# Fourteen expert steps of the second layer moved into the later groups of the second attention

## The reference, cut to what matters

```python
# attention, 16 heads of 8 rows a batch; q, k, v are (b, h, dh=8, t=256) views of the projections
attn = softmax(einsum('bhdt,bhds->bhts', k, v) * temperature)
out  = einsum('bhdt,bhts->bhds', q, attn)
x = x + ga * out
h = layernorm(x) * (1 + cb) + sb
# experts: 8 routed and one shared, 176 hidden rows each; two experts a token are weighted, the rest 0
g = einsum('th,ehi->eti', h, w_gate); u = einsum('th,ehi->eti', h, w_up)
eo = einsum('eti,eih->eth', silu(g) * u, w_down)
x = x + gb * (einsum('te,eth->th', combine, eo) + sigmoid(h @ shared_gate) * so)
```

## Time and profile before

| | |
|---|---|
| median of three runs | 473.43 us |
| profiled execution | 476.3 us |
| its span | 474.5 us, 7765 instructions |
| TensorE products, busy | 426.4 us, 90% |
| VectorE, busy | 360.9 us, 76% |
| ScalarE, busy | 336.2 us, 71% |
| GpSimd, busy | 252.9 us, 53% |
| mean granted TensorE clock | 0.845 |

### The profile page before, as it was taken

The page is one execution under the profiler, slowest core; times in us unless marked ns, Lnnn a source line. Parts: engine busy times, 40 slices in busy tenths (PEclk is TensorE's granted clock), DMA queues, the critical chain, the costliest instruction groups (busy, mean ns, idle before and its releaser), DMA issues.

```text
span 474.5 us, 7765 instructions
## 1 busy us (share of the span) xinstructions
PE 426.4 (90%) x2212; PEld 285.5 (60%) x2212; DVE 360.9 (76%) x891; ACT 336.2 (71%) x898; POOL 252.9 (53%) x276
## 2 busy tenths in 40 slices
PE   8979778899899899886999889969989999999995
PEld 6667666676567677652433335324447887787883
DVE  4766795867898879689858896995848777879763
ACT  3364558787688686778998889968946566585552
POOL 3302238786866776822443543443418964766663
PEclk9997998999999999995565555555569999999999
DMA  6730021121134643633058344203114342433640
GB/s 185 207 112 2 0 79 57 44 92 56 35 114 108 164 149 103 123 87 114 12 90 118 96 98 131 60 5 102 24 22 149 127 126 81 141 128 92 183 130 22
DMA packets 45675, 44.68 MB, mean 94 GB/s; under 512 B 5557, under 2 KB 33789, under 8 KB 45633
## 3 DMA queue, kind: packets, MB, share of 16 engines
q1 hardware_dynamic: 45632, 44.19, 34.5%
HBM read 37.73 MB, written 6.44 MB: 93 GB/s over the span
## 4 chain that ended last, share of the span: by engine, by line
PE 43%; DVE 13%; issue 5%; ACT 3%; POOL 1%; POOLq 0%; DVEq 0%; ACTq 0%
PE P L1244 8%; PE P L1245 8%; PE P L1246 8%; PE P L1523 8%; PE P L1513 5%; DVE nm L902 4%; PE P L1380 1%; ACT EX L1179 1%; POOL hidl L469 1%; PE P L1349 1%; PE P L1268 1%; DVE O L917 1%; PE P L1374 1%; DVE kvs L697 1%; DVE SC L606 1%
## 5 line engine op out<-in xcount | busy, mean ns | idle before, releaser
L469 POOL TENSOR_TENSOR hidl<-tmp,hidh 128x512 fp32r<-128x512 f32 x116 | 149.3, 1296 | 76.6 <-ACT hidh L1131 73.9
L1179 ACT ACTIVATE EX<-P,nm 128x256 f32<-128x256 f32 x256 | 116.9, 496 | 12.5 <-DVE nm L902 12.2
L1131 ACT ACTIVATE hidh<-tmp 128x512 fp32r<-128x512 f32 x116 | 73.1, 630 | 44.8 <-DVE tmp L865 20.4
L902 DVE TENSOR_REDUCE nm<-P 128x4 f32<-128x1024 f32 x64 | 77.8, 1218 | 24.4 <-PE P L1513 24.0
L1523 PE MATMUL P<-EX,qs 128*32 128x256 f32 x512 | 66.8, 619 | 12.1 <-DVE O L917 12.0
L1244 PE MATMUL P<-XH,WH 128*128 128x512 f32 x176 | 76.1, 433 | 1.5 <-DVE tmp L974 0.6
L1245 PE MATMUL P<-XH,WL 128*128 128x512 f32 x176 | 70.1, 399 | 0.0
L1246 PE MATMUL P<-XL,WH 128*128 128x512 f32 x176 | 70.1, 398 | 0.0
L513 POOL TENSOR_TENSOR qs<-qT,rz 128x128 f32<-128x128 f32 x64 | 24.6, 406 | 81.5 <-DVE rz L910 81.5
L865 DVE TENSOR_TENSOR tmp<-P,G 128x512 f32<-128x512 f32 x64 | 43.6, 687 | 25.2 <-ACT P L1152 20.1
L1244 PE MATMUL P<-hidh,WH 128*128 128x512 f32 x124 | 50.7, 409 | 11.3 <-POOL hidl L469 9.8
(11 more groups left out here) (138 smaller groups left out, 670.7 us busy)
## 6 DMA issues: line engine op xcount, KB each, us to landing
G<-gate_rows SPq DMA_DIRECT2D x56, 256.0 KB, 3.3
kv_parts<-kvs SPq DMA_DIRECT2D x16, 256.0 KB, 2.4
VS<-kv_parts SPq DMA_DIRECT2D x48, 64.0 KB
KS<-kv_parts SPq DMA_DIRECT2D x48, 64.0 KB
G<-gate_rows SPq DMA_DIRECT2D x8, 224.0 KB, 3.0
G<-gate_rows SPq DMA_DIRECT2D x8, 192.0 KB, 3.3
G<-gate_rows SPq DMA_DIRECT2D x8, 160.0 KB, 2.6
X<-in_x SPq DMA_DIRECT2D x4, 256.0 KB, 2.9
```

Of the source, the lines that this page charges most:

```text
L469: nc.gpsimd.tensor_tensor(hidl[:, u % 3, :], source, hidh[:, u % 3, :].bitcast(fp32), ALU.subtract).then_inc(s["low_ready"], 1)
L902: v.tensor_reduce(nm1[:, g % 4, 2 * h:2 * h + 2, :], P[:, bank:bank + 2, :].rearrange("p j (h s) -> p (j h) s", h=2), AX.X, ALU.max, negat ...
L1131: sc.activation(hidh[:, u % 3, :], source, ACT.Copy).then_inc(s["high_ready"], 1)
L1179: last = sc.activation(ex1(g, j)[:, h * S:(h + 1) * S], P[:, bank_s1(g, j), h * S:(h + 1) * S], ACT.Exp, bias=nm1[:, g % 4, j, h:h + 1], a ...
```

## The change

Groups 18 to 31 of the attention (from GF = 18) each take one expert step along; MERGED = 14 steps, all 13 of pair 0 and the first of pair 1. In these steps SiLU is written as (tanh(g/2) + 1) x g x 0.5 and then times up: a tanh on ScalarE (`tanh1`) and two three-operand instructions on VectorE (`silu1`, `up1`), the multiplication with the router's weight on GpSimd (`gated`), and the down product as one product in full fp32 (`down_whole`, with the staged weights and without split). From group 18 on the scores have four banks, one for each j, and the maxima are taken bank by bank (`maxima1`, four a group in place of two); banks 4 and 7 are for gate and up. Copies of the context go to ScalarE from group 16 on. To be ready, the weight loads and splits move forward (quarters at groups 2 to 5, 7 to 10, 12 to 15), and so do the layer norm and the router of pairs 0 and 1 (13 to 18 in place of 15 to 25). The other 38 steps stay as they were, behind the attention. `exps_ready`, `maxima_done`, `used1` and `split1` hold the new counts.

```diff
 LAG = 4
+GF = 18
...
+
+        hidf = EX[:, 0, 0:2, :]
...
+        spare = [kvs[:, r, :, :].rearrange("p o d -> p (o d)").bitcast(fp32) for r in range(KVR)]
+        th = spare[0:2]
+        t1 = spare[2]
+        hidm = [spare[3], kvf[:, :, :, :].rearrange("p k o d -> p (k o d)")]
...
             load_experts_1(0)
+            load_experts_1(1)
             attention_out(0)
             kv_load(2)
-            load_experts_1(1)
+            load_experts_1(2)
             attention_out(1)
             kv_store(3)
             attention_out(2)
             kv_load(3)
-            load_experts_1(2)
-            attention_out(3)
-            attention_out(B - 4)
-            attention_out(B - 3)
             gates_store(NP)
             for n in range(GR):
                 gate_load(NP * E + n)
-            attention_out(B - 2)
-            attention_out(B - 1)
+            attention_out(3)
             for n in range(GR, NP * C1):
                 p, i = divmod(n, C1)
-                if p == 0 and i == 9:
-                    gates_store(NP + 1)
-                if p >= 2 and i == 0:
+                if n in (6, 10, 14, 18):
+                    attention_out(B - 4 + n // 4 - 1)
+                if i == 0:
                     gates_store(NP + p)
                 gate_load(NP * E + n)
...
+            def gated(m):
+
...
+                pool.wait_ge(s["u_read"], m + 1)
+                pool.wait_ge(gate_in[q % GR], gates_loaded(q))
+                if m >= 2:
+                    pool.wait_ge(s["down_done"], NP * STEPS0 + m - 1)
+                nc.gpsimd.tensor_tensor(hidm[m % 2], t2[:, m % 2, :], G[:, q % GR, :], ALU.mult
+                                        ).then_inc(s["bc_read"], 1)
...
-                if g in (15, 15 + GPP):
-                    root(3, (g - 15) // GPP)
+                if g in (13, 13 + GPP):
+                    root(3, (g - 13) // GPP)
                 queries(g)
...
-                    clear(1)
...
+                for w, quarters in enumerate(((2, 3, 4, 5), (7, 8, 9, 10), (12, 13, 14, 15))):
...
+                    clear(g // 5)
+                for p in range(3):
                     i = g - GPP * p
-                    if i in (10, 12):
...
+                    if i in (9, 11):
+                        attention_residual(2 * p + (i - 9) // 2)
+                    if i == 15 and p < 2:
...
+                if g >= GF:
+                    gated(g - GF)
+            root(3, 2)
+            for n in range(MERGED, NP * C1):
                 p, i = divmod(n, C1)
-                low_part(NP * STEPS0 + n, hidf[:, n % 2, :])
...
+            def maxima1(g, j):
+
+                dve.wait_ge(s["s1_ps"], HPG * g + j + 1)
+                v.tensor_reduce(nm1[:, g % 4, j, :], P[:, bank_s1(g, j), :].rearrange("p (h s) -> p h s", h=2),
+                                AX.X, ALU.max, negate=True).then_inc(s["nm1_ready"], 1)
+
+            def silu1(m):
+
+                dve.wait_ge(s["gact_ready"], m + 1)
+                v.scalar_tensor_tensor(out=t1, in0=th[m % 2], scalar=1.0, in1=P[:, BANK_GM, :],
+                                       op0=ALU.add, op1=ALU.mult).then_inc(s["t1_done"], 1)
+
+            def up1(m):
+
+                dve.wait_ge(s["t1_done"], m + 1)
+                dve.wait_ge(s["u_ps"], m + 1)
+                if m >= 2:
+                    dve.wait_ge(s["bc_read"], used1(m - 1))
+                v.scalar_tensor_tensor(out=t2[:, m % 2, :], in0=t1, scalar=0.5, in1=P[:, BANK_UM, :],
+                                       op0=ALU.mult, op1=ALU.mult).then_inc(s["u_read"], 1)
+
             def denominators(g):
                 dve.wait_ge(s["e1_ready"], HPG * (g + 1))
...
+                if 3 <= g < GF:
                     outputs(g - 3)
-                if g + 1 < NG:
+                if g + 1 < GF:
                     maxima(g + 1, 0)
+                elif g + 1 < NG:
+                    maxima1(g + 1, 0)
                 if g == 0:
                     gate_experts(0, NP - 1)
                 if g >= 1:
                     denominators(g - 1)
+                if g > GF:
+                    silu1(g - 1 - GF)
+                if GF <= g + 1 < NG:
+                    maxima1(g + 1, 1)
+                if g > GF:
+                    up1(g - 1 - GF)
+                if GF <= g + 1 < NG:
+                    maxima1(g + 1, 2)
                 if g < 2:
                     kv(2 * TPP + 2 + g)
                 if g == 2:
...
-                    kv((NP - 1) * TPP + (10, 11, 13, 14).index(g))
+                if g in (9, 10, 12, 15):
...
+                    if i == 13:
                         ln_stats(3, p)
+                    if i == 14:
+                        ln_apply(3, p)
+                    if i == 18:
+                        router_weights(1, p, 2)
+                if g == NG - 1:
+                    ln_stats(3, 2)
+                if g + 1 < GF:
+                    maxima(g + 1, 1)
+                elif g + 1 < NG:
+                    maxima1(g + 1, 3)
+                for p in range(2):
+                    i = g - GPP * p
...
                         router_logits(1, p)
...
+                    if i == 17:
+                        router_weights(1, p, 0)
+                        router_weights(1, p, 1)
             denominators(NG - 1)
...
+            silu1(MERGED - 1)
+            up1(MERGED - 1)
...
+            dve.wait_ge(s["c1_ps"], NG - 3)
+            dve.wait_ge(s["bc_read"], used1(MERGED))
+            for n in range(MERGED, NP * C1):
...
+            def outputs(g):
+                b = g // GPB
+                act.wait_ge(s["c1_ps"], g + 1)
...
+                sc.activation(O[:, b % 2, g % GPB, :], P[:, BANK_C1, 0:S], ACT.Copy).then_inc(s["o1_ready"], 1)
+
+            def tanh1(m):
...
+                act.wait_ge(s["g_ps"], m + 1)
...
+                    act.wait_ge(s["t1_done"], m - 1)
+                sc.activation(th[m % 2], P[:, BANK_GM, :], ACT.Tanh, scale=0.5).then_inc(s["gact_ready"], 1)
...
+                    if j == 0 and g in (17, 17 + GPP):
+                        router_exp(1, (g - 17) // GPP)
+                    if j == 1 and g >= GF - 1:
+                        outputs(g - 2)
                     if j == HPG - 1:
+                        if g >= GF:
+                            tanh1(g - GF)
...
+                        if g in (15, 15 + GPP):
+                            modulate(3, (g - 15) // GPP)
+                            high_input(1, (g - 15) // GPP)
                         if g in (18, 18 + GPP):
...
+                            weights_out(1, (g - 18) // GPP)
+            outputs(NG - 2)
...
+            def gate1(m):
+
+                p, i = divmod(m, C1)
+                if i == 0:
+                    pe.wait_ge(s["xl_ready"], NP + p + 1)
+                claim(BANK_GM, "t1_done", m + 1)
+                split_mm(BANK_GM, i * D, D, XH[:, p % 2, :], XL[:, p % 2, :], True, True).then_inc(s["g_ps"], 1)
+
...
+                claim(BANK_UM, "u_read", m + 1)
+                split_mm(BANK_UM, FP + i * D, D, XH[:, p % 2, :], XL[:, p % 2, :], True, True).then_inc(s["u_ps"], 1)
...
+                pe.wait_ge(s["bc_read"], used1(m + 1))
+                mm(P[:, bank_y1[p], :], stage1[:, i * D:(i + 1) * D], hidm[m % 2], start=(i == 0), stop=(i == C1 - 1)
+                   ).then_inc(s["down_done"], 1)
...
+                if g < GF - 1:
...
+                else:
+                    if g + 1 < NG:
+                        score(g + 1, 0)
+                    context(g - 2, 0)
+                    context(g - 2, 1)
+                    if g + 1 < NG:
+                        score(g + 1, 1)
+                    if g >= GF:
+                        if g == GF:
+                            pe.wait_ge(s["w1_low"], 12)
+                        gate1(g - GF)
+                    if g + 1 < NG:
+                        score(g + 1, 2)
+                    if g >= GF:
+                        up1(g - GF)
+                    if g + 1 < NG:
+                        score(g + 1, 3)
+                    if g >= GF + 2:
+                        down_whole(g - GF - 2)
...
+                    if i == 15:
+                        transpose_tokens(3, p, misc_x(1, p))
+                    if i == 16:
                         route(1, p)
-                    if i == 25:
+                    if i == 18:
                         weights_back(1, p)
...
+            for h in range(2):
+                context(NG - 2, h)
+            gate_up(MERGED)
+            down_whole(MERGED - 2)
+            for h in range(2):
+                context(NG - 1, h)
+            gate_up(MERGED + 1)
+            down_whole(MERGED - 1)
...
+BANK_GM = 4
+BANK_UM = 7
...
+    return 2 * ((2 * g + j // 2) % 3) + j % 2 if g < GF else j
```

201 lines of the change are left out of this document (98 added, 103 removed).

## The result

The changed kernel took 513.39 us in the median of four runs (506.54 to 529.73), the kernel before 473.01 in the same session. The forecast was 468.8 us.

What follows compares the result with a forecast made beforehand. TensorE was taken to bound both the attention, because of its half clock, and the expert steps behind it. -30.6 + 21.0 + 5.0 = -4.6 us on 473.4 gave 468.8 us; 456 to 487 us was to hold four fifths.

Steps and rivals of the forecast that it cites:

- The step that failed is the clock: Merged groups from 18: full clock after the first two groups and staying; 8.2 us a group if it does not rise.
- the forecast was 87.2: Group 18 to step 14: 77.2 us of turns + 6.5 between + 3.5 exit = 87.2 us, where 66.2 stood.
- The reason behind it: TensorE work without a gap raises the clock, read from two rises; a merged group gives 5.4 us at half clock.
- the clock keeps falling: Rival: merged turns where router work or ScalarE's waits idle TensorE run at half clock, 2.85 us dearer each; chance 0.23.
- all eleven, 500 us: The falling-clock rival's upper case: all eleven further merged turns at half clock give 500 us; with six, 486 us.
- Scores: TensorE in merged groups: four scores follow each other after 0.43 us at full clock, so 0.9 us a group.
- The turn at full clock: One merged group at full clock, set by loops of waits: 5.35 us, with TensorE's own sum at 4.4 us.
- two loops of waits: Merged turn at full clock: ScalarE's loop through the context copy 5.2 us, VectorE's and TensorE's through single banks 5.25 us.
- The pieces between: Pair 1's router in turns 21 to 26, on VectorE, TensorE and ScalarE, adds 6.5 us to the merged part.
- Before the merged part: Before group 18: pair 0's router pieces 3 us and SyncE's queue 2, together +5.0, ends 0 and 11.
- Removed steps: Behind the attention: 14 of 52 expert steps leave, at 2.19 us each, saving 30.6 us.
- Tanh's table: ScalarE in merged steps: tanh shares the exponential's table, 0 us; if not, 36 us.

Runs made afterwards that it cites:

- e14: e12 with pair 1's router pieces on ScalarE back behind head 1 of a group, copies and tanh still later; 486.32 us.
- e17: e12 with the scores in two pairs whose matmuls alternate between two heads, both banks claimed first; 470.38 us.
- e12: e11 with TensorE's order put back to the change's own, four single-bank scores between the products; 480.81 us.
- e5: The change with one swap in SyncE's queue, batch 1's attention results ahead of the third weight load; 524.83 us.
- e7: e6 with every merged gate product issued twice as filler; 494.19 us.
- e8: e6 with every merged gate and up product issued twice as filler; 496.02 us.
- e6: The change with four adjacent scores, ScalarE's copy and tanh a group later, pair 1's transpose-dependent pieces moved, and e5's swap; 485.93 us.
- e3: The kernel before with both score calls of a group adjacent, ahead of both context halves; 471.79 us.
- e11: e6 with pair 1's router pieces on ScalarE behind the last head, third weight part behind the last maximum, weights back a group later; 471.40 us.
- e10: The change with merged down products shortened to 128 of 512 tokens, except in the first step of a pair; 511.99 us.
- e15: e13 with 8 merged expert steps in place of 14; 475.86 us.
- e13: e11 with pair 0's router pieces on ScalarE later, GpSimd's `low_input` one group later and SyncE's queue reordered; 467.32 us.
- e16: e13 with three heads' keys and values of pair 2 fetched ahead of batch 1's results instead of two; 465.53 us.

## Why the prediction was wrong

**The step that failed is the clock**: "I take it that the clock is up after the first two groups and stays up." In the change's profile it was at half when the merged part began and first rose at 386.1 us, 92 us later. The merged stretch had 129.7 us at half clock. At (9.9 - 5.7) / 9.9 = 0.42 us lost for each, that is 54 us, and 139.5 - 54 = 85 us is what the stretch would take at full clock: the forecast was 87.2. The executions agree: between spans of 527.9 and 504.7 us (clock 0.795 and 0.843) half-clock time differs by 58 us and the span by 23, 0.40 each.

**The reason behind it did not hold.** The forecast took gapless work as what raises the clock, from two rises. The trace of before already had longer gapless stretches without a rise, which the prediction did not look at; this is one of its windows inside the attention, and one of the change (columns of the earlier trace rows):

```profile
290.00:300.00 10.00, 10.00 (x68) 5.13 (x68) 6.82 (x11) 9.37 (x43) 5.32 (x9) 0.50 0.38 109
```

```profile
330.00:340.00 10.00, 10.00 (x33) 4.74 (x32) 5.04 (x11) 4.63 (x18) 2.04 (x3) 0.50 0.11 26
```

In the change TensorE had no wait from 303.4 to 351.2 us, and stayed at half; so did e14 for 28.6 us (its stretches):

```profile
300.00:328.60 28.60, 28.59 (x105) 14.08 (x108) 14.03 (x33) 17.18 (x65) 8.55 (x12) 0.50 0.29 82
```

What does decide when it rises is open. It came 3.5 us after group 19's first maximum with the scores woven (e17), 16 us after it in e12, 35 in e14, whose work is the same up to that point, 21 in e5, and 92 in the change. With filler the rise that lasted until the router pieces came 19 us after it in both e7 and e8, for 25 in e6. These are single profiles, and e12 and e14 show how far two of the same work lie apart.

**The rival "the clock keeps falling" has the right size, for a reason that is only partly its own**; it had 0.23. In the change's profile no wait made the clock fall, it never rose: the first wait for the router's transposes came at 351 us, at half clock. Where it had risen (e5, e6) it fell at the place that the rival named, the router pieces and ScalarE's waits. Its price was 2.85 us a turn and measured 4.2. The missing 1.35 is 1.7 on the half-clock side (9.9 for 8.2: scores 2.9 for 1.5, split products behind a score 3.2 for 2.7) less 0.35 on the full-clock side (5.7 for 5.35). So even its "all eleven, 500 us" was too low. The Trainium skill (TensorE: Matmul & The Clock Gate, HAM oscillation) says that products in bursts between waits are throttled anew each time. e6's two stretches are such a case, a wait of 2.7 us and then half clock; the 47.8 us of the change at half clock without a wait are not.

**Scores.** Priced by starts 0.43 us apart for four matmuls, which were two heads side by side. That price belongs to adjacent heads, and the change takes adjacency away. e17 shows it: 7 to 10 us, in part because the clock rose earlier in its profile. The Trainium skill (TensorEngine Tiling (Array Packing), Key Properties) has different tiles of the array run in parallel; the traces agree where heads stand side by side with their banks free (two in 0.73 us in before, four in 0.82 in e3, at half clock).

**The turn at full clock** was near in size, but in the change's own order not for the reason given, and that is luck. The forecast had TensorE at 4.4 us and two loops of waits at 5.2 and 5.25. In e5 a turn is 5.7 us, TensorE is busy for 5.68 of them and its chain holds nothing else: four scores cost 4 x 0.43 us for the 0.9 taken, and the product after the first split one behind a score starts 0.43 to 0.50 us later, for 0.23. The loops do lead where TensorE has less to do: in e11 (4.9 to 5.9 us a turn) and in e10, where a turn at full clock went from 5.7 to 5.3 us and its chain through VectorE. With the waits gone and the clock up from 308.5 us (e12) the stretch from group 19 to step 14 takes 381.0 - 292.2 = 88.8 us, for 87.2.

**The pieces between** were put at 6.5 us. In e6 the three router groups took 30.3 us against 3 x 5.35, 14 too many, 13 of them for where ScalarE's pieces stand; in e11 they cost 1.

**Before the merged part**: 5.0 forecast, 11.3 measured (93.5 for 82.2), just beyond its ends of 0 and 11; group 18 itself, which carries the first two of pair 0's three weight parts, has 1.8 of it (6.6 for 4.8). Of the rest 3.0 us are the statistics of group 14 waiting for batch 1 (7.6 us for 4.6), 4.3 the router's groups 16 and 17 (5.0 and 7.4 for 4.0 and 4.1). The direction was named, and the first of these is SyncE's order as it was named, at 3 us for 2. That curing it by the order alone puts the stores behind 24 small fetches was not foreseen.

**Removed steps**: 30.6 forecast, 26.8 measured (94.3 for 121.1). The forecast priced the 14 that leave at the mean of all 52. In before they took 381.49 - 353.36 = 28.1 us, and the 38 that stay take 1.3 us more than they did. e15 gives six steps back and is 8.5 us slower than e13 by the medians, 1.4 each, for 1.3 expected. (In the change's profile the attention also starts 4.4 us earlier, 200.6 for 205.0; e3, which differs from before only inside the attention, starts 2.1 us earlier, so that this is not all the change's doing. With it the parts add up: -4.4 + 11.3 + 73.3 - 26.8 = 53.4 us between the spans.) **Tanh's table**: 0, as taken.

Open: what makes the clock rise, and how much of the step from the change to e14 (some 20 us or more) is the later copy and how much the router pieces that moved with it. With the copy later and the pieces left, ScalarE would wait for transposes that wait for the copy; this was not tried.

## What to carry to other kernels

When work is merged into a part that runs at half clock, price every turn at both levels, and before you count on a rise look for stretches of the same kind that did not bring one. Then ask which wait will drop the clock; here it was a rare piece (the router) whose consumer has the main loop's instructions queued behind it. Place such a piece where the next round's work is already through that queue: with four adjacent scores this cost nothing and was worth 14.5 us, with single ones no gain is shown. A price read from neighbours that share an engine holds only while they stay neighbours. A mean over all steps is not the price of the first ones.

## What the runs showed of the hardware

TensorE can be busy for 28.59 of 28.60 us and be granted half clock throughout (e14), and for 47.76 of 47.80 in the change. Three quarters off an fp32 product's columns shortened the turn at half clock from 9.9 to 8.6 us, with no gain in the kernel's time that its spread would show (e10). Score matmuls on 24 rows, at half clock: one head alone 0.72 us, two neighbours 0.73 to 0.79 (before, e17), four 0.82 (e3), and 0.79 us from first to second where the second head's bank comes free later (e1). Four stores of attention rows took 3.3 us to the fetch back with the last of 12 small fetches issued 5 us ahead (e13), 5.9 behind 18 (e16) and 13.6 right behind 24 (e11). The clock fell 0.6 us behind a wait of 2.7 us in e6 and 9.4 us behind one in e5; behind a wait of 0.7 us in e14 it stayed up.
